# An attention and mixing block on one core: the order of the work behind the last scores, written out anew for all five queues

## What is computed

```
x = x + layernorm(attention(layernorm(x)))
x = x + layernorm(channel_mix(layernorm(x)))

attention(x):    q, k, v = split(x @ w_qkv);  softmax(q k^T / 16) v @ out_w^T + out_b
channel_mix(x):  x_prev = x shifted by one row (zero ahead of the first)
                 xr = mu_r x + (1 - mu_r) x_prev;   xk = mu_k x + (1 - mu_k) x_prev
                 sigmoid(xr @ W_r^T) * (relu(xk @ W_k^T)^2 @ W_v^T)
```

## Time and profile before

| | us |
|---|---|
| median of 3 runs | 801.1 |
| lowest and highest of them | 798.98, 801.8 |
| the profiled execution's own time | 799.6 |
| its span, first to last instruction | 797.8 |
| TensorE busy | 784.1 (98% of the span) |
| VectorE busy | 647.8 (81%) |
| ScalarE busy | 573.5 (72%) |
| GpSimd busy | 529.3 (66%) |

### The profile page before, as it was taken

How to read it: one execution, slowest core, us unless ns; L and a number is a source line. 1 busy time by engine, 2 the same in 40 slices (tenths; PEclk the granted TensorE clock), 3 DMA queues, 4 the chain that set the end, 5 groups by cost and what they waited for, 6 DMA issues and landing times.

```text
span 797.8 us, 16563 instructions
## 1 busy us (share of the span) xinstructions
PE 784.1 (98%) x5823; PEld 576.6 (72%) x5823; DVE 647.8 (81%) x1677; ACT 573.5 (72%) x791; POOL 529.3 (66%) x768
## 2 busy tenths in 40 slices
PE   8999999999999999999999999999999999999996
PEld 6556777777777777777777777777777777777884
DVE  6788888877797879888878879987778787788787
ACT  4677768777677778777668787887767676775663
POOL 3370356666767768866756776966675985677776
PEclk9999999999999999999999999999999999999999
DMA  6798789477866769867657986957876554777701
GB/s 186 158 186 125 138 159 177 87 143 147 172 119 141 148 126 189 146 126 139 94 141 157 183 156 130 138 110 145 145 140 123 108 108 106 147 146 143 149 29 40
DMA packets 348260, 108.70 MB, mean 136 GB/s; under 512 B 321937, under 2 KB 347921, under 8 KB 348177
## 3 DMA queue, kind: packets, MB, share of 16 engines
q1 hardware_dynamic: 348176, 107.64, 70.0%
HBM read 18.75 MB, written 8.39 MB: 34 GB/s over the span
## 4 chain that ended last, share of the span: by engine, by line
PE 94%; DVE 2%; DMA 0%; issue 0%; POOL 0%; POOLq 0%; ACT 0%; DVEq 0%
PE Y L1725 7%; PE Y L1729 7%; PE Y L1727 7%; PE Y L1726 7%; PE Y L1728 7%; PE S L1704 7%; PE S L1708 7%; PE S L1705 7%; PE S L1707 7%; PE S L1706 7%; PE M L1669 6%; PE M L1670 6%; PE M L1671 6%; PE M L1687 1%; PE M L1688 1%; PE M L1685 1%
## 5 line engine op out<-in xcount | busy, mean ns | idle before, releaser
L1285 DVE TENSOR_SCALAR_CACHE_REDUCE probs<-S 128x512 f32<-128x512 f32 x256 | 173.2, 677 | 65.0 <-PE S L1708 64.8
L933 ACT ACTIVATE probs<-probs,exp_bias,kappa 128x2048 f32<-128x2048 f32 x64 | 133.9, 2092 | 60.1 <-DVE exp_bias L1298 60.1
L1303 DVE TENSOR_TENSOR p_lo<-probs,p_hi 128x2048 f16<-128x2048 f32 x61 | 166.7, 2732 | 5.7 <-ACT p_hi L862 5.7
L1727 PE MATMUL Y<-pt_hi,planes 128*128 128x256 f16 x496 | 135.2, 273 | 0.0
L1725 PE MATMUL Y<-pt_hi,planes 128*128 128x256 f16 x496 | 135.2, 273 | 0.0
L1726 PE MATMUL Y<-pt_lo,planes 128*128 128x256 f16 x496 | 135.2, 273 | 0.0
L1728 PE MATMUL Y<-pt_lo,planes 128*128 128x256 f16 x496 | 135.2, 273 | 0.0
L1729 PE MATMUL Y<-pt_hi,planes 128*128 128x256 f16 x496 | 135.2, 273 | 0.0
L862 ACT ACTIVATE p_hi<-probs 128x2048 f16<-128x2048 f32 x64 | 121.4, 1897 | 8.8 <-DMA pt_hi<-p_hi 4.8
L1704 PE MATMUL S<-turned,q_hi 128*128 128x512 f16 x256 | 97.0, 379 | 1.6 <-DMA turned<-planes 1.6
L1708 PE MATMUL S<-turned,q_lo 128*128 128x512 f16 x256 | 97.0, 379 | 0.0
(11 more groups left out here) (289 smaller groups left out, 2039.9 us busy)
## 6 DMA issues: line engine op xcount, KB each, us to landing
x_res<-in_L_attn_x SPq DMA_DIRECT2D x32, 256.0 KB, 3.6
out_x<-gate SPq DMA_DIRECT2D x31, 256.0 KB, 3.2
xs<-in_L_attn_x SPq DMA_DIRECT2D x13, 512.0 KB, 4.9
pt_hi<-p_hi SPq DMA_TRANSPOSE x62, 5.0
pt_lo<-p_lo SPq DMA_TRANSPOSE x62, 4.8
xs<-in_L_attn_x SPq DMA_DIRECT2D x2, 256.0 KB, 3.8
gate<-in_L_attn_x SPq DMA_DIRECT2D x1, 512.0 KB, 6.5
att<-in_L_attn_x SPq DMA_DIRECT2D x1, 512.0 KB, 4.3
```

The source lines that it names most:

```text
L1285: dve.tensor_scalar(probs[:, h % 2, t, c * BLK:(c + 1) * BLK], S[k % RING][:, :], 1.0, None, ALU.mult, ALU.max, accum_out=chunk_max[:, t, ...
L1303: dve.tensor_tensor(p_lo[:, t, :], probs[:, h % 2, t, :], p_hi[:, t, :], ALU.subtract).then_inc(p_lo_made, 1)
L1727: pe.matmul(to[:, 1, :], high, p_h, start=False, stop=False, skip_group_check=True)
```

## The change

It replaces the lists of steps behind the main loop on all five queues. The main loop and every step's own code stay. Some steps change their engine, where both have a version of it: the four `differences` of H-5 to H-2 go from GpSimd to VectorE; `split_low(H - 6, 0)`, `split_low(H - 4, 1)`, `squares_low(H - 6)`, `add_attention(H - 4)`, `finish(H - 5)` and `add_attention_tile(0)` go the same way; `squares_low(H - 5)`, `add_attention` of H-3 and H-2 and `finish(H - 7)` go from VectorE to GpSimd. VectorE's norms `mix_in(H - 5)`, `attention_norm` of H-4 and H-3 and `gate_norm(H - 4)` go to ScalarE, and so the matching roots on GpSimd get shifts. The rest moves within its list. The diff, in the order sync queue, GpSimd, ScalarE, VectorE, TensorE:

```diff
@@ -493,4 +493,4 @@
             turn_low(H - 2, 1)
-            load_residual(H - 3)
             turn_high(H - 2, 1)
+            load_residual(H - 3)
             store(H - 8)
@@ -498,4 +498,4 @@
             turn_low(H - 1, 0)
-            load_residual(H - 2)
             turn_high(H - 1, 1)
+            load_residual(H - 2)
             turn_low(H - 1, 1)
@@ -818,35 +818,29 @@
             squares_low(H - 7)
-            res_rsqrt(H - 5, 0)
+            res_rsqrt(H - 5, H - 4)
             split_low(H - 6, 1)
-            split_low(H - 6, 0)
-            att_rsqrt(H - 4, 0)
-            add_attention(H - 4)
-            differences(H - 5)
-            res_rsqrt(H - 4, H - 4)
-            squares_low(H - 6)
+            att_rsqrt(H - 4, H - 3)
+            res_rsqrt(H - 4, H - 3)
             split_low(H - 5, 1)
+            att_rsqrt(H - 3, H - 2)
             gate_rsqrt(H - 7, H - 6)
-            att_rsqrt(H - 3, 0)
+            finish(H - 7)
+            add_attention(H - 3)
+            squares_low(H - 5)
+            res_rsqrt(H - 3, H - 2)
             gate_rsqrt(H - 6, H - 5)
-            differences(H - 4)
             finish(H - 6)
-            res_rsqrt(H - 3, H - 3)
-            split_low(H - 4, 1)
-            att_rsqrt(H - 2, H - 3)
+            att_rsqrt(H - 2, H - 1)
             gate_rsqrt(H - 5, H - 4)
-            differences(H - 3)
-            finish(H - 5)
-            res_rsqrt(H - 2, H - 2)
+            add_attention(H - 2)
             split_low(H - 3, 1)
-            gate_rsqrt(H - 4, 0)
+            res_rsqrt(H - 2, H - 1)
             split_low(H - 3, 0)
-            differences(H - 2)
+            gate_rsqrt(H - 4, H - 3)
             finish(H - 4)
-            att_rsqrt_tile(0, H - 2)
+            att_rsqrt_tile(0, H - 0)
             att_rsqrt_tile(1, 0)
-            add_attention_tile(0)
             add_attention_tile(1)
-            res_rsqrt_tile(0, H - 1)
+            res_rsqrt_tile(0, H - 0)
             res_rsqrt_tile(1, 0)
-            gate_rsqrt(H - 3, H - 3)
+            gate_rsqrt(H - 3, H - 2)
             differences_tile(1)
@@ -1117,45 +1111,49 @@
             probs_high(H - 1, 0)
-            probs_high(H - 1, 1)
+            mix_norm(H - 5, H - 4)
+            attention_norm(H - 4, H - 3)
             mix_in_out(H - 5)
+            probs_high(H - 1, 1)
             carry(H - 5)
             attended_high(H - 3)
-            squares(H - 6)
             split_high(H - 5, 1)
+            mix_norm(H - 4, H - 3)
+            mix_in_out(H - 4)
+            squares(H - 6)
             receptance(H - 6)
-            mix_norm(H - 4, H - 4)
+            attention_norm(H - 3, H - 2)
             gate_norm(H - 7, H - 6)
+            split_high(H - 5, 0)
             squares(H - 5)
-            mix_in_out(H - 4)
             carry(H - 4)
-            split_high(H - 5, 0)
-            gate_norm(H - 6, H - 5)
-            attended_high(H - 2)
             split_high(H - 4, 1)
-            mix_norm(H - 3, H - 3)
-            split_high(H - 4, 0)
+            attended_high(H - 2)
             receptance(H - 5)
+            mix_norm(H - 3, H - 2)
+            gate_norm(H - 6, H - 5)
+            split_high(H - 4, 0)
+            mix_in_out(H - 3)
+            carry(H - 3)
             squares(H - 4)
-            attention_norm(H - 2, H - 3)
+            attention_norm(H - 2, H - 1)
             receptance(H - 4)
-            mix_in_out(H - 3)
+            split_high(H - 3, 1)
             gate_norm(H - 5, H - 4)
-            carry(H - 3)
             split_high(H - 3, 0)
-            split_high(H - 3, 1)
-            mix_norm(H - 2, H - 2)
+            mix_norm(H - 2, H - 1)
             attended_high(H - 1)
             mix_in_out(H - 2)
-            carry(H - 2)
+            gate_norm(H - 4, H - 3)
             squares(H - 3)
             receptance(H - 3)
-            attention_norm_tile(0, H - 2)
+            carry(H - 2)
+            attention_norm_tile(0, H - 0)
             squares(H - 2)
             receptance(H - 2)
-            mix_norm_tile(0, H - 1)
+            mix_norm_tile(0, H - 0)
             mix_in_out_tile(0)
             mix_in_out_tile(1)
-            gate_norm(H - 3, H - 3)
+            gate_norm(H - 3, H - 2)
             squares_tile(0)
-            squares_tile(1)
             receptance_tile(0)
+            squares_tile(1)
             receptance_tile(1)
@@ -1596,28 +1594,29 @@
             mix(H - 6, 0)
-            inverse_sums(H - 1)
             attention(H - 4)
             attention_stats(H - 4)
-            mix_in(H - 5)
+            inverse_sums(H - 1)
+            split_low(H - 6, 0)
             probs_low(H - 1, 0)
-            attention_norm(H - 4)
+            add_attention(H - 4)
             residual_stats(H - 4)
-            probs_low(H - 1, 1)
-            attended_low(H - 3)
+            differences(H - 5)
             mix(H - 5, 1)
-            gated(H - 7)
-            gated_stats(H - 7)
+            attended_low(H - 3)
+            probs_low(H - 1, 1)
             attention(H - 3)
             attention_stats(H - 3)
-            gated(H - 6)
+            gated(H - 7)
+            gated_stats(H - 7)
+            squares_low(H - 6)
             mix(H - 5, 0)
-            attention_norm(H - 3)
+            differences(H - 4)
+            mix(H - 4, 1)
+            gated(H - 6)
             gated_stats(H - 6)
-            finish(H - 7)
-            squares_low(H - 5)
-            add_attention(H - 3)
+            split_low(H - 5, 0)
             residual_stats(H - 3)
+            split_low(H - 4, 1)
             attended_low(H - 2)
-            mix(H - 4, 1)
-            split_low(H - 5, 0)
             mix(H - 4, 0)
+            gated(H - 5)
             attention(H - 2)
@@ -1625,9 +1624,9 @@
             split_low(H - 4, 0)
-            gated(H - 5)
+            differences(H - 3)
             gated_stats(H - 5)
+            mix(H - 3, 1)
+            mix(H - 3, 0)
             squares_low(H - 4)
-            add_attention(H - 2)
             residual_stats(H - 2)
-            mix(H - 3, 0)
-            mix(H - 3, 1)
+            finish(H - 5)
             gated(H - 4)
@@ -1635,6 +1634,6 @@
             attended_low_tile(0)
-            gate_norm(H - 4)
+            differences(H - 2)
             attended_low_tile(1)
-            attention_tile(0)
             mix(H - 2, 1)
+            attention_tile(0)
             attention_tile(1)
@@ -1642,2 +1641,3 @@
             mix(H - 2, 0)
+            add_attention_tile(0)
             attention_norm_tile(1)
@@ -1651,5 +1651,5 @@
             mix_tile(1, 0)
-            mix_tile(1, 1)
-            gated_stats(H - 2)
             mix_tile(0, 0)
+            gated_stats(H - 2)
+            mix_tile(1, 1)
             mix_tile(0, 1)
@@ -1961,3 +1961,2 @@
             mix_keys(H - 6, 0)
-            receptance(H - 6)
             values(H - 3, 4, 5)
@@ -1965,22 +1964,21 @@
             values(H - 3, 5, 8)
-            feed(H - 7)
-            values(H - 2, 0, 2)
+            receptance(H - 6)
+            values(H - 2, 0, 1)
             project_out(H - 3, KEYS_LEFT)
-            values(H - 2, 2, 3)
-            feed(H - 6)
-            mix_keys(H - 5, 0)
-            values(H - 2, 3, 4)
             turn_mix_in(H - 4)
+            feed(H - 7)
+            values(H - 2, 1, 4)
+            mix_keys(H - 5, 0)
+            feed(H - 6)
             values(H - 2, 4, 8)
+            receptance(H - 5)
             feed(H - 5)
-            values(H - 1, 0, 1)
             project_out(H - 2, KEYS_LEFT)
-            receptance(H - 5)
-            mix_keys(H - 4, 0)
             turn_mix_in(H - 3)
-            values(H - 1, 1, 2)
+            mix_keys(H - 4, 0)
+            values(H - 1, 0, 2)
             receptance(H - 4)
-            values(H - 1, 2, 4)
+            values(H - 1, 2, 5)
             feed(H - 4)
-            values(H - 1, 4, 8)
+            values(H - 1, 5, 8)
             turn_mix_in(H - 2)
@@ -1997,5 +1995,5 @@
             keys_tile(0)
-            keys_tile(1)
-            feed_tile(0)
             receptance_tile(0)
+            feed_tile(0)
+            keys_tile(1)
             receptance_tile(1)
```

More of the change, by code:

```diff
@@ L493, in _ @@
             turn_low(H - 2, 1)
+            turn_high(H - 2, 1)
             load_residual(H - 3)
-            turn_high(H - 2, 1)
             store(H - 8)
@@ L498, in _ @@
             turn_low(H - 1, 0)
+            turn_high(H - 1, 1)
             load_residual(H - 2)
-            turn_high(H - 1, 1)
             turn_low(H - 1, 1)
@@ L1596, in _ @@
             mix(H - 6, 0)
-            inverse_sums(H - 1)
             attention(H - 4)
             attention_stats(H - 4)
-            mix_in(H - 5)
+            inverse_sums(H - 1)
+            split_low(H - 6, 0)
             probs_low(H - 1, 0)
-            attention_norm(H - 4)
+            add_attention(H - 4)
             residual_stats(H - 4)
+            differences(H - 5)
+            mix(H - 5, 1)
```

(56 more changed lines are left out.)

8 lines of the change are left out of this document (4 added, 4 removed).

## The result

The changed kernel takes 802.66 us (median of 20 runs, 800.83 to 804.07), the kernel before 800.94 (20 runs beside it): the ratio is 1.0019, with a 95% interval of 1.0011 to 1.0027. The forecast for the median was 800.7 us, 0.4 less than before. The kernel became slower instead: 1.7 us by the two medians, 1.5 us by the ratio. The loss is real and small, inside what the prediction called "the same", but of the other sign.

A forecast was written before the change was run, and what follows sets the result against it. TensorE was taken as the bound up to about 775 us, with 3.0 us idle. Terms 0 + 0 - 0.75 + 0.35 = -0.4 us gave a median of 800.7 us, range 798.5 to 803.0.

The forecast's parts named there:

- the same: Outcome class for the whole kernel: time within 0.3% (2.4 us) of the kernel before; chance 0.89.
- Part 1: TensorE's matmul steps reordered between 733 and 771 us: inputs arrive in time, cost 0, bounds 0 and +1.5 us.
- TensorE stops for a transpose: Rival at turn_mix_in(H-4): a late transpose landing stalls TensorE; 802.2 us if milder, 804.1 if late; chance 0.17.
- the milder case: At turn_mix_in(H-4): transpose landing at 739.1 gives +1.5 us, median 802.2; such milder stalls held chance 0.12.
- Part 2: Differences moved from GpSimd to VectorE, four norms from VectorE to ScalarE: cost 0 by themselves.
- Part 3: Step at 776.45, keys of H-2: TensorE's 0.9 us wait goes; term -0.75 us, bounds -0.9 and +0.15.
- VectorE held up at 773 us: Rival: finish(H-4) on GpSimd delays mix(H-2, 1); +0.15 there, +0.5 with the last steps, 801.6 us; chance 0.25.
- the prediction's own sign (1.5 or more): Test at the mixes for the keys of H-2: mix(H-2, 1) taking 1.5 us or more shows Part 3 wrong.
- Part 4: Last six matmul steps: feed 1 starts 5.3 to 5.7 us after keys 0, against 5.24; +0.35, bounds 0 and +0.5.

The follow-up runs named there:

- e4: The changed kernel with both p_lo subtractions of block H-1 issued as four operations of 512 columns each; ratio 1.0005 to the kernel before.
- e5: The changed kernel with both p_lo in quarters and the last tile's steps put back to the order before the change; ratio 1.0000 to the kernel before.
- e3: The changed kernel with VectorE's first p_lo, probs_low(H-1, 0), moved behind mix(H-5, 1); ratio 1.0008 to the kernel before.
- e7: The changed kernel with p_lo in quarters, finish(H-4) later on GpSimd, and the old order of the last tile; ratio 0.9992 to the kernel before.
- e6: The changed kernel with p_lo in quarters and GpSimd's finish(H-4) behind the second square root of the last block's attention; ratio 1.0002 to the kernel before.
- e8: The kernel before, order untouched, with both p_lo of block H-1 in four operations each; ratio 0.9998 to the kernel before.

## Why the prediction was wrong

The sum was -0.4 us and the ratio says +1.5 (0.0019 x 801). By its own steps:

- **Part 1, the matmul steps reordered: forecast 0, measured +1.84 at the end of all values, of which 1.78 arise at turn_mix_in(H-4).** This is the step that failed. The place in time was right: wanted at 742.0, 14.4 us behind the first projection, and 14.42 is where it runs once nothing holds it. The failed sentence is that "the other input, the shift from GpSimd, is done by 738.5", and its price of 1.75 us for four small instructions. The shift was done at 744.73, which is 742.6 on the time scale of the kernel before, 4.1 us later than that. The four instructions took 4.33 us (740.40 to 744.73), of which rshift's stall is 2.0. The prediction took their price from a block where they ran behind the p_lo, clear of it, and asked of GpSimd's operations only how long they are. It did not ask what VectorE runs at that moment. arstd took 2.74 us and rshift 2.22, and each lies on the chain. VectorE also lost 1.60 us waiting for the norm that arstd had delayed, which made add_attention(H-4) late. The landing of the transpose, on which the prediction built its rival, was foreseen well (0.98 us earlier against 0.84) and was not the limit: in the changed kernel p_hi ran at 739.14 without a wait for it.
- **The rule was at hand.** The prediction weighed the Trainium skill ("SBUF — State Buffer", "Who interferes with whom"), that the loser of the port pair blocks fully, saw the trace agree for the difference of 2.51 us, and applied it to part 3 alone. The same rule, laid over part 1, says that an operation of two columns waits for the rest of the p_lo just as one of 512 does. The rows show that (2.74 us for the power, 2.51 for the difference), and the quarters show that the wait shrinks with the instruction.
- **The rival "TensorE stops for a transpose"** had the place, the sign and the size (+1.5 for the milder case, 802.2 us for the median against the measured 802.66), and got 0.12 for the wrong cause. That its size fits is luck: it was worked out from a late landing, and the landing was early.
- **Part 2, cost 0:** incomplete in the same way. Moving attention_norm(H-4) to ScalarE adds ashift to the chain (0.20 us alone, 0.62 beside a quarter), and the norm itself takes 1.09 us there against 0.72 on VectorE. rshift of H-4 is in both kernels. What this move costs by itself no run shows. ScalarE itself had room (9.11 and 7.54 of 12 us busy, idle before mix_norm).
- **Part 3: forecast -0.75, measured -0.44.** The wait before the keys of H-2 went, but the one for sq_lo(H-3) is 0.70, where some 0.2 was forecast. Mixes at 777.27 took 1.53 us beside finish(H-4) at 776.92, which was the mechanism of the rival "VectorE held up at 773 us" and, by the prediction's own sign (1.5 or more), shows this part wrong; yet the outcome lies between its forecast and that rival's +0.15. From the end of all values to the keys of tile 0 the changed kernel goes from 1.84 to 1.40 us late. With the stall of part 1 taken out (e4) it is the same: from 0.25 us late to 0.19 ahead of the kernel before.
- **Part 4: forecast +0.35, measured +0.12** (5.36 against 5.24). Against e5, where at the end only the order differs, it is +0.31. The chain was right: keys 1 starts 3.29 us behind keys 0 (3.2 to 3.6 was said), feed 1 5.36 (5.3 to 5.7 was said). The term stood high in that range, which holds +0.06 to +0.46.
- **The chances.** "Same" within 0.3% held the result at 1.0019. The range did hold 802.66, by a rival whose cause did not happen. The sign was wrong: the sum put part 1 at the friendly end of its own bounds (0 and +1.5), and a reordering under a full TensorE could only lose there.

The parts as measured close the sum: 1.84 - 0.44 + 0.12 = 1.52 us.

What stays open: what the move of the norms costs without the p_lo beside it, and what makes the clock fall at the end of some executions and not of others.

## What to carry to other kernels

Where one engine is full, a step that is moved earlier is safe only if every instruction on its input chain is priced with what runs on the engine it shares a resource with at that moment. A tiny operation on GpSimd is not tiny if it starts behind a long two-input operation on VectorE: its price is the rest of that operation, and a chain with two such operations can pay it twice. Started 0.12 us ahead of it, the same operation paid nothing, so a trace in which it was short is no promise. The remedy that costs no place in the order is to cut the long instruction into pieces. Moving it elsewhere helped in one place (e3) and in the other took one wait away and made two (e2).

## What the runs showed of the hardware

A 128x2 multiplication on GpSimd took 0.20 us alone and 2.22 when it started 0.11 us behind VectorE's subtraction of 128x2048. The power of 128x2 took 0.70 alone, 0.75 when it started 0.12 us ahead of that subtraction, 2.74 when it started 0.12 us behind it, and 1.14 beside its quarters.

Behind the first keys of the last block TensorE's granted clock fell in six of the twelve profiled executions (the starred rows), whatever the order of the end. Windows of the changed kernel with quarters (columns as in the earlier trace rows), and below of the kernel before with quarters:

```profile
784.00:786.00 2.00, 0.94 (x8) 0.94 (x8) 2.00 (x4) 1.09 (x2) 1.86 (x3) 1.00 0.01 4
786.00:788.00 2.00, 1.73 (x6) 1.23 (x6) 1.82 (x8) 0.89 (x2) 0.61 (x3) 0.51 0.35 124
788.00:790.00 2.00, 2.00 (x8) 1.68 (x7) 1.32 (x5) 0.47 (x1) 1.41 (x3) 0.64 0.02 7
```

```profile
784.00:786.00 2.00, 0.43 (x3) 0.43 (x4) 1.97 (x5) 1.43 (x3) 1.76 (x4) 1.00 0.02 4
786.00:788.00 2.00, 2.00 (x11) 1.73 (x10) 1.83 (x7) 0.87 (x2) 0.83 (x2) 0.56 0.11 39
788.00:790.00 2.00, 2.00 (x10) 1.85 (x9) 1.83 (x8) 0.84 (x3) 1.18 (x3) 0.59 0.26 92
```

It was full until 786 us, and in the 2 us before, TensorE had been busy for 0.94 and 0.43 us. That alone does not decide it: the profiles of the kernel before and of e7 have 0.33 and 0.50 us there and stayed at the full clock until the last feed. In the two that fell, it was granted between 0.51 and 0.64, about the lower of its two levels (1.2 of 2.4 GHz), for some 3 us and then full again. The receptance of tile 0 took 2.08 us instead of 1.13. In e4, e6 and e8 the last feed comes 1.1 to 1.4 us later behind the first keys than in the like kernel at full clock (6.79, 6.45 and 6.30 us against 5.36, 5.36 and 5.24). This is as large as the effect of the change, so profiles of this kernel are compared by positions ahead of that stage. It also goes with the spread between executions of one kernel: of the 90 of the kernel before that were timed beside the experiments, the 35 with a mean clock of 0.998 or more have a median of 799.8 us, the 41 at 0.996 or 0.997 one of 800.8, and the 14 below that one of 802.3.
